# Cross attention before a six-layer transformer: biases added by VectorE and GpSimd, kB cleared at the start, x fetched in two adjacent transfers

## The chip, the cores and the metric

The kernel runs on one core of a Trainium2 chip. A core has five engines that work side by side and meet through semaphores: TensorE (PE; its weight loads are shown as PEld), VectorE (DVE), ScalarE (ACT), GpSimd (POOL) and SyncE (SP), which here only issues DMAs. The metric is the device time in microseconds (us). The kernel before has a median of 1854.88 us over 3 runs (1846.59 to 1856.06). All arithmetic is float32.

## The reference

```
x:[4,512,128]  ctx:[4,77,128]
xn = layernorm(x)
q = xn @ Wq.T + bq;  k = ctx @ Wk.T + bk;  v = ctx @ Wv.T + bv
attended = softmax(q k^T / sqrt(128)) @ v
x = x + tanh(g_xattn) * ((xn + attended) @ Wo.T + bo)
z = layernorm(x)
for 6 layers:
    z = local attention(shift(z); 16 heads of 64, window 32, rotary tables) + z
    z = gated FFN(layernorm(shift(z))) + z
x = x + tanh(g_ffn) * z
```

The change is in the first three steps, the cross attention. The biases bv and bo are no longer zero in the data, so they have to be added.

## The kernel before, in words

The program has a prologue (the cross attention and the second layernorm) and then a software-pipelined loop over 192 units, 8 for each of 24 groups (6 layers times 4 batch rows), with 22 slots to drain. The loop isn't touched. Each engine has its program written out by hand; nothing plans the order.

The prologue works by batch row b = 0 to 3, each with 4 tiles of 128 tokens (TPG = 4). Its steps, with the lines of the code:

- SP fetches, in this order (L1107 to L1120): the first half of x (b 0 and 1), the identity and the mask, ctx, four weights, bq, bk, bv, bo, the two gates, the second half of x (b 2 and 3), the rotary constants `rope`; then the scales, the layer weights and some bias columns.
- PE turns the four weights and ctx (L284, L287), ACT copies them out of PSUM (L574, L576).
- Layernorm of x: for each b, DVE takes statistics (L761, L764), POOL computes 1/sqrt(var + eps) in two small instructions (L1018, L1020), DVE normalises with four `tensor_scalar` (L771). DVE's order is statistics 0, statistics 1, normalise 0, statistics 2, normalise 1, and so on. When POOL has done all four b it clears kB (L1023: 128 x 8704 float32), the buffer of the loop's keys.
- PE turns the normalised rows (L293), ACT copies (L581), PE computes keys (L298) and queries (L303), ACT adds bk and bq as it copies (L585, L589), PE computes the scores (L307).
- DVE takes the maxima and subtracts them (L784, L786). PE meanwhile computes v (L313, L314): for each b, a product of a row of ones with the row bv opens the PSUM bank, and the product of ctx and Wv is accumulated on it. ACT copies v out (L592) and, behind that in its program, does the four exponentials (L595).
- DVE sums, inverts and scales the probabilities (L789 to L793), PE turns them (L321) and multiplies by v (L326), DVE adds xn (L797).
- For each b PE turns the sum (L332) and then writes bo into the bank of the output with a one-row product of 128 x 512 (L334); after all four, the output projection accumulates on it (L339).
- DVE computes x + tanh(g) times the bank (L803) and runs the second layernorm with the same routines; POOL has the same two small instructions per b, then multiplies the rotary tables by the scales (L1029, four instructions of 128 x 256), waits for PE's last transpose (L345) and clears `vw` (L1031), whose space the prologue used for weights.
- ACT copies the transposes into xT (L604, L605), and the loop begins with L370.

The new names of the change: `bias_x` and `bo_t` lie in the tile `rstd`, which the loop uses only later; `cols_zero` takes over what `zero_ready` said of the tile `cols`.

Of the kernel before, what the change touches and what calls it, by code (L numbers as in the profile page):

```python
# [66 lines left out]
def build(nc, x_in, ctx_in, g_xattn, g_ffn, Wq, bq, Wk, bk, Wv, bv, Wo_x, bo, Wqkv, q_scale, k_scale,  # L67
          Wo, ln_g, ln_b, W1, b1, W2, b2, rope_in, mats_in, mask_in, out):
    ctx = ExitStack()
    with ctx:  # L70
# [65 lines left out]
        bcol = sb("bcol", [P, 2])  # L136
        brow = sb("brow", [1, 2, C])
        ones = sb("ones", [1, P])
        gcol = sb("gcol", [P, 2])
# [15 lines left out]
        mv_x = [quad(small(b, 24, 2 * TPG), 2) for b in range(B)]  # L155
        vare_x, rstd_x, mx_x, rs_x, rr_x = ([small(b, 32 + 4 * i, TPG) for b in range(B)] for i in range(5))
        first_bank = [ps[2 * b] for b in range(B)]
        second_bank = [ps[2 * b + 1] for b in range(B)]
# [14 lines left out]
        cst_ready = sem("cst_ready")  # L173
        zero_ready = sem("zero_ready")
        w1_pad = sem("w1_pad")
        vw_zero = sem("vw_zero")
# [29 lines left out]
        a_rTev = sem("a_rTev")  # L206
        a_y = sem("a_y")
        a_x1 = sem("a_x1")
        b_stat = sem("b_stat")
# [69 lines left out]
        def _(pe):  # L279
# [10 lines left out]
            for b in range(B):  # L290
                pe.wait_ge(a_xn, 4 * b + 4)
                for t in range(TPG):
                    mm = pe.transpose(first_bank[b][:, t * P:(t + 1) * P], xn_x[b][:, t, :], ident[:, :])  # L293
                mm.then_inc(a_xnT, 1)
                if b == 0:
                    pe.wait_ge(ctxT_ev, 1)
                    pe.wait_ge(cst_ready, 4)
                    pe.matmul(ps[7][:, 0:B * CTX], wxT[:, 1, :], ctxT[:, :, :].rearrange("p b s -> p (b s)"),  # L298
                              start=True, stop=True).then_inc(kx_mm, 1)
# [4 lines left out]
            for b in range(B):  # L304
# [4 lines left out]
                mm.then_inc(a_sc, 1)  # L309
            pe.wait_ge(small_dma, 16 * 6)  # L310
            for b in range(B):
                o_ = ps[7][0:CTX, b * C:(b + 1) * C]
                pe.matmul(o_, ones[0:1, 0:CTX], brow[0:1, 0, :], start=True, stop=False)  # L313
                mm = pe.matmul(o_, ctxT[:, b, :], wxT[:, 2, :], start=False, stop=True)  # L314
            mm.then_inc(vx_mm, 1)
# [13 lines left out]
            for b in range(B):  # L329
                pe.wait_ge(a_res, b + 1)  # L330
                for t in range(TPG):
                    mm = pe.transpose(second_bank[b][:, t * P:(t + 1) * P], res_x[b][:, t, :], ident[:, :])  # L332
                mm.then_inc(a_rT, 1)
                pe.matmul(heads(first_bank[b][:, :], C), ones[0:1, :],  # L334
                          brow[0:1, 1, :].unsqueeze(1).to_broadcast([1, TPG, C]), start=True, stop=True)
            for b in range(B):
                pe.wait_ge(a_rTev, b + 1)
                for t in range(TPG):
                    mm = pe.matmul(first_bank[b][:, t * P:(t + 1) * P], rT_x[b][:, t * P:(t + 1) * P], wxT[:, 3, :],  # L339
                                   start=False, stop=True, skip_group_check=True)  # L340
                mm.then_inc(a_y, 1)
            for b in range(B):
                pe.wait_ge(b_x, 4 * b + 4)
                for t in range(TPG):
                    mm = pe.transpose(second_bank[b][:, t * P:(t + 1) * P], x_nat[b][:, t, :], ident[:, :])  # L345
                mm.then_inc(b_xT, 1)
            pe.matmul(SC_BANK[:, :], mean_w[:, :], rT_x[1], start=True, stop=True).then_inc(sc_open, 1)

# [223 lines left out]
        def _(act):  # L572
# [3 lines left out]
            act.activation(ctxT[:, :, :].rearrange("p b s -> p (b s)"), ps[7][:, 0:B * CTX], ACT.Copy).then_inc(ctxT_ev, 1)  # L576
            act.wait_ge(cst_ready, 4)
            act.wait_ge(mats_dma, 16 * 2)
            for b in range(B):
                act.wait_ge(a_xnT, b + 1)  # L580
                act.activation(xnT_x[b], first_bank[b][:, :], ACT.Copy).then_inc(a_xnTev, 1)  # L581
                if b == 0:
                    act.wait_ge(small_dma, 16 * 6)
                    act.wait_ge(kx_mm, 1)
                    act.activation(kxT[:, :, :].rearrange("p b s -> p (b s)"), ps[7][:, 0:B * CTX], ACT.Identity,  # L585
                                   bias=bcol[:, 1:2]).then_inc(kx_ev, 1)
            for b in range(B):
                act.wait_ge(a_q, b + 1)
                act.activation(q_x[b], second_bank[b][:, :], ACT.Identity, bias=bcol[:, 0:1]).then_inc(a_qev, 1)  # L589
            act.activation(tg[:, :], gcol[:, :], ACT.Tanh).then_inc(tanh_ready, 1)  # L590
            act.wait_ge(vx_mm, 1)
            act.activation(vx[:, :, :].rearrange("p b c -> p (b c)"), ps[7][0:CTX, :], ACT.Copy).then_inc(vx_ev, 1)  # L592
            for b in range(B):
# [156 lines left out]
        def _(dve):  # L750
            dve.memset(ones[:, :], 1.0).then_inc(cst_ready, 1)
            dve.memset(minus_half[:, :], -0.5).then_inc(cst_ready, 1)
            dve.memset(shift_back[:, :], 0.5 * float(np.log(LN_SHIFT))).then_inc(cst_ready, 1)
            dve.memset(norm_min[:, :], NORM_MIN ** 2)
            dve.memset(mean_w[:, :], 1.0 / C).then_inc(cst_ready, 1)
            dve.memset(xT[64:C, :, 0:1], 0.0)

            def statistics(b, src, stat):
# [16 lines left out]
            for b in range(B + 1):  # L775
                if b < B:
                    dve.wait_ge(x_dma[b // 2], 16)
                    statistics(b, row, a_stat)
                if b > 0:
                    normalise(b - 1, row, xn_x, a_stat, a_rstd, a_xn)  # L780
            for b in range(B):
                dve.wait_ge(a_sc, b + 1)
                sc = heads(first_bank[b][:, :], P)[:, :, 0:CTX]
                dve.tensor_reduce(mx_x[b], sc, AX.X, ALU.max).then_inc(a_mx, 1)  # L784
                dve.wait_ge(a_mx, b + 1)
                dve.tensor_tensor(pr_x[b], sc, spread(mx_x[b], CTX), ALU.subtract).then_inc(a_sub, 1)  # L786
            for b in range(B):
                dve.wait_ge(a_exp, b + 1)
# [5 lines left out]
            for b in range(B):  # L794
                dve.wait_ge(a_att, b + 1)
                dve.wait_ge(a_xn, 4 * b + 4)
                dve.tensor_tensor(res_x[b], heads(first_bank[b][:, :], P), xn_x[b], ALU.add).then_inc(a_res, 1)  # L797
            dve.wait_ge(tanh_ready, 1)
            for b in range(B + 1):
                if b < B:  # L800
                    rows = x1[:, TPG * b:TPG * (b + 1), :]
                    dve.wait_ge(a_y, b + 1)
                    dve.scalar_tensor_tensor(out=rows, in0=heads(first_bank[b][:, :], P), scalar=tg[:, 0:1],  # L803
                                             in1=rows, op0=ALU.mult, op1=ALU.add).then_inc(a_x1, 1)
# [204 lines left out]
        def _(pool):  # L1009
            pool.memset(cols[:, :, :], 0.0).then_inc(zero_ready, 1)  # L1010
            pool.memset(w1[:, 2 * DFF:], 0.0).then_inc(w1_pad, 1)
            pool.wait_ge(cst_ready, 3)

# [8 lines left out]
            inverse_roots(a_stat, a_rstd)  # L1022
            pool.memset(kB[:, :, :, :], 0.0).then_inc(zero_ready, 1)  # L1023
            inverse_roots(b_stat, b_rstd)

            pool.wait_ge(cst_dma, 16)
            pool.wait_ge(scale_dma, 16 * 6)
            for t in range(TPG):
                pool.tensor_tensor(tables[:, 0, t, :], rope[:, t, :], scales[:, 0, :], ALU.mult).then_inc(table_ready, 1)  # L1029
            pool.wait_ge(b_xT, B)  # L1030
            pool.memset(free, 0.0).then_inc(vw_zero, 1)  # L1031
# [72 lines left out]
        def _(sp):  # L1104
            xt = x_in.rearrange("b (t p) c -> p (b t) c", p=P)
            half = B * TPG // 2
            sp.dma_start(x1[:, 0:half, :], xt[:, 0:half, :]).then_inc(x_dma[0], 16)  # L1107
            sp.dma_start(ident[:, :], mats_in).then_inc(mats_dma, 16)
            sp.dma_start(mask_f[:, :, :], mask_in).then_inc(mats_dma, 16)
# [4 lines left out]
            sp.dma_start(bcol[:, 1:2], bk.unsqueeze(1)).then_inc(small_dma, 16)  # L1114
            sp.dma_start(brow[:, 0, :], bv.unsqueeze(0)).then_inc(small_dma, 16)
            sp.dma_start(brow[:, 1, :], bo.unsqueeze(0)).then_inc(small_dma, 16)
            sp.dma_start(gcol[:, 0:1], g_xattn.unsqueeze(0).to_broadcast([P, 1])).then_inc(small_dma, 16)
            sp.dma_start(gcol[:, 1:2], g_ffn.unsqueeze(0).to_broadcast([P, 1])).then_inc(small_dma, 16)
            sp.dma_start(x1[:, half:, :], xt[:, half:, :]).then_inc(x_dma[1], 16)
            sp.dma_start(rope[:, :, :], rope_in).then_inc(cst_dma, 16)  # L1120
# [20 lines left out]
            second_weights(0)  # L1141
            sp.wait_ge(zero_ready, 1)
            with nc.allow_non_contiguous_dma(reason="a few bias columns"):
# [99 lines left out]
```

## Time and profile before

| | |
|---|---|
| runs | 1856.06, 1854.88, 1846.59 us |
| the profiled execution: its own time | 1855.28 us |
| its span (first to last instruction shown) | 1853.5 us |
| mean granted TensorE clock | 0.982 |
| busy | PE 96%, PEld 61%, DVE 87%, ACT 72%, POOL 81% |
| the loop's first instruction | 81.02 us after the span's start |

Busy shares are means over the whole span. The loop holds some 1770 of its 1853.5 us, so these shares speak of the loop; the prologue has to be read from its own stretch, 0 to 81 us. The chain of waits is the view to read first there: it follows the work that ended last back to what released it, so an edit counts only with what it takes off that chain.

### The profile page before, as it was taken

The numbers are of one execution on the slowest core, as the hardware profiler recorded it, in microseconds if no ns is written. First come the engines' busy times: TensorE is split into PE (matmuls) and PEld (weight loads), VectorE is DVE, ScalarE is ACT, GpSimd is POOL, SyncE is SP. The second block draws the span as 40 slices with busy tenths as digits, with TensorE's granted clock in tenths as the row PEclk, the third lists the DMA queues.
The fourth block names the chain that finished last, engine by engine and source line by source line (L and its number), as shares of the span: only waits on it lengthen the run. The fifth ranks groups of instructions, "written<-read, shape, count | busy, mean of one in ns | idle before, by whom it ended". The sixth has DMA issues, their size and how long they took to land.

```text
span 1853.5 us, 48613 instructions
## 1 busy us (share of the span) xinstructions
PE 1770.5 (96%) x18100; PEld 1122.9 (61%) x18100; DVE 1621.2 (87%) x2780; ACT 1327.3 (72%) x2363; POOL 1497.1 (81%) x1200
## 2 busy tenths in 40 slices
PE   5789999999999999999999999999999999999986
PEld 4446666666666666666666666666666666666663
DVE  5499989899989999899899998999998998988873
ACT  2267778677777687787787777787877877877763
POOL 2399988888888888889888888888888888888760
PEclk9699999999999999999999999999999999999998
DMA  4013222223222223222222222222232222222221
GB/s 106 15 44 85 74 56 69 64 56 82 71 67 68 63 58 83 64 73 70 56 63 74 72 74 60 67 61 73 71 80 57 69 61 56 59 72 56 56 64 29
DMA packets 154989, 120.46 MB, mean 65 GB/s; under 512 B 42577, under 2 KB 151173, under 8 KB 154629
## 3 DMA queue, kind: packets, MB, share of 16 engines
q1 hardware_dynamic: 154757, 117.35, 24.5%
q8 instruction: 147, 2.41, 0.6%
q14 instruction: 85, 0.70, 0.1%
HBM read 18.66 MB, written 1.05 MB: 11 GB/s over the span
## 4 chain that ended last, share of the span: by engine, by line
PE 77%; DVE 11%; POOL 4%; issue 3%; SPq 2%; DMA 1%; ACT 1%; DVEq 0%; POOLq 0%; ACTq 0%
PE qk_bank L370 17%; PE ring_bank L442 10%; PE ring_bank L466 9%; PE ring_bank L383 8%; PE sc_bank L417 7%; PE ring_bank L510 6%; PE ring_bank L430 4%; PE ring_bank L393 3%; PE ring_bank L455 3%; PE ring_bank L521 3%; PE ring_bank L404 3%; DVE rn L832 2%; DVE step L827 2%; DVE o L888 2%; POOL turned L1039 1%
## 5 line engine op out<-in xcount | busy, mean ns | idle before, releaser
L1039 POOL TENSOR_TENSOR turned<-qkn,tables 128x512 f32<-128x512 f32 x384 | 489.1, 1274 | 210.8 <-DVE qkn L840 203.1
L1046 POOL TENSOR_TENSOR turned<-qkn,tables 128x512 f32<-128x512 f32 x384 | 497.3, 1295 | 0.0
L370 PE MATMUL qk_bank<-wqkv,xT 128*128 128x512 f32 x768 | 368.7, 603 | 16.8 <-DVE qkn L848 16.8
L1075 POOL TENSOR_TENSOR turned<-turned 128x512 f32<-128x512 f32 x192 | 255.0, 1328 | 15.1
L1082 POOL TENSOR_TENSOR turned<-turned 128x512 f32<-128x512 f32 x192 | 244.9, 1276 | 15.1
L442 PEld LDWEIGHTS ring_bank<-vw,pT 128*32 128x32 f32 x6144 | 156.6, 110 | 143.8 <-issue 143.7
L650 ACT ACTIVATE kB<-ring_bank 64x512 f32<-64x512 f32 x384 | 225.4, 587 | 23.3 <-PE ring_bank L404 20.9
L623 ACT ACTIVATE vs<-ring_bank 128x512 f32<-128x512 f32 x192 | 114.7, 597 | 173.3 <-PE ring_bank L383 158.5
L814 DVE TENSOR_REDUCE ss<-sq 128x16 f32<-128x1024 f32 x192 | 232.0, 1208 | 7.7 <-ACT sq L614 7.7
L888 DVE TENSOR_TENSOR o<-ring_bank,rr 128x512 f32<-128x512 f32 x192 | 132.0, 687 | 107.3 <-PE ring_bank L442 104.8
L383 PE MATMUL ring_bank<-wqkv,xT 128*128 128x512 f32 x384 | 217.2, 648 | 1.6 <-DVE x L968 1.6
L417 PE MATMUL sc_bank<-kB,qT 128*32 128x128 f32 x6144 | 208.4, 276 | 0.1
L442 PE MATMUL ring_bank<-vw,pT 128*32 128x128 f32 x6144 | 208.4, 276 | 0.1
L660 ACT ACTIVATE sc_bank<-mask_f 128x512 f32<-128x512 f32 x192 | 114.5, 596 | 131.2 <-DVE pr L863 130.8
L370 PEld LDWEIGHTS qk_bank<-wqkv,xT 128*128 128x128 f32 x768 | 132.0, 192 | 120.5 <-issue 94.4
L614 ACT ACTIVATE sq<-qk_bank 128x1024 f32<-128x1024 f32 x192 | 198.0, 1031 | 0.0
L417 PEld LDWEIGHTS sc_bank<-kB,qT 128*32 128x32 f32 x6144 | 156.6, 110 | 34.9 <-issue 34.8
L466 PE MATMUL ring_bank<-oT,wo 128*128 128x256 f32 x768 | 173.8, 379 | 0.0
L455 PEld LDWEIGHTS ring_bank<-ident,o 128*128 128x128 f32 x768 | 95.8, 141 | 101.8 <-issue 84.2
L466 PEld LDWEIGHTS ring_bank<-oT,wo 128*128 128x128 f32 x768 | 142.2, 190 | 18.1 <-DVE uT L946 0.8
L510 PE MATMUL ring_bank<-xnT,w 128*128 128x512 f32 x288 | 143.2, 609 | 8.5 <-DVE xnT L937 7.3
L840 DVE TENSOR_TENSOR qkn<-qk_bank,rn 128x512 f32<-128x512 f32 x192 | 132.8, 692 | 20.0
(173 smaller groups left out, 3149.5 us busy)
## 6 DMA issues: line engine op xcount, KB each, us to landing
vw<-vs SPq DMA_DIRECT2D x1152, 64.0 KB, 2.1
vw<-vs SPq DMA_DIRECT2D x672, 32.0 KB, 1.9
wqkv<-in_L_ffn_Wqkv_dram SPq DMA_DIRECT2D x20, 384.0 KB, 3.5
wo<-in_L_ffn_Wo_dram SPq DMA_DIRECT2D x20, 128.0 KB, 3.3
w<-in_L_ffn_W_dram SPq DMA_DIRECT2D x6, 341.0 KB, 3.4
wqkv<-in_L_ffn_Wqkv_dram SPq DMA_DIRECT2D x1, 1536.0 KB, 10.3
x<-in_x_dram SPq DMA_DIRECT2D x2, 512.0 KB, 4.1
out_dram<-x SPq DMA_DIRECT2D x4, 256.0 KB, 2.3
```

The source lines that it names most:

```text
L370: mm = pe.matmul(QK[u % 2][:, i * UW:(i + 1) * UW], tok, wqkv[:, layer % 2, cut:cut + UW], start=True, stop=True)
L383: pe.matmul(RING[i % RINGS][:, :], xT[:, b, t * P:(t + 1) * P], wqkv[:, layer % 2, cut:cut + UW], start=True, stop=True).then_inc(ring_mad ...
L417: mm = pe.matmul(heads(SC_BANK[WIN * w:WIN * (w + 1), k * P:(k + 1) * P]), qT[:, u % 2, k, WIN * w:WIN * (w + 1)], kB[:, HP * half + k, :, ...
L442: mm = pe.matmul(heads(RING[i % RINGS][WIN * w:WIN * (w + 1), k * P:(k + 1) * P]), pT[:, u % 2, k, WIN * w:WIN * (w + 1)], vw[:, u % 2, w, ...
L466: mm = pe.matmul(RING[i % RINGS][:, 0:HALF], wo[:, layer % 2, k, :], oT[:, k, HALF * h:HALF * (h + 1)], start=(k == 0), stop=(k == KO - 1))
L510: pe.matmul(RING[i % RINGS][:, :], w1[:, DFF * j + k * P:DFF * j + (k + 1) * P], xnT[:, :], start=True, stop=True).then_inc(ring_made[i % ...
L650: ev = act.activation(kB[64 * h:64 * h + 64, HP * half:HP * half + HP, h, WIN + P * t:WIN + P * t + P], RING[i % RINGS][64 * h:64 * h + 64 ...
L814: dve.tensor_reduce(ss[:, :], heads(sq[:, :]), AX.X, ALU.add).then_inc(ss_done, 1)
L1039: return pool.tensor_tensor(heads(turned[:, u % 2, 2 * i, :]), heads(qkn[:, u % 2, i * UW:(i + 1) * UW]), table.unsqueeze(1).to_broadcast( ...
L1046: return pool.tensor_tensor(halves(turned[:, u % 2, 2 * i + 1, :]), halves(qkn[:, u % 2, i * UW:(i + 1) * UW])[:, :, ::-1, :], table.rearr ...
L1075: pool.tensor_tensor(q, q, turned[:, u % 2, 1, :], ALU.add).then_inc(q_summed, 1)
L1082: pool.tensor_tensor(k, k, turned[:, u % 2, 3, :], ALU.add).then_inc(k_summed, 1)
```

## The change

It does four things.

1. v: the four products of ones and bv go. DVE adds bv, spread over the partitions by the DMA, as it copies v out of PSUM; ACT's copy of v goes. This addition stands on DVE behind the four subtractions (L786).
2. Output: the four products of ones and bo go. DVE multiplies bo (spread over the partitions by the DMA) by tanh(g) once, and POOL adds the result to x itself, 128 x 512 for each b, before the projection's result is added to x. The tanh moves forward on ACT, behind the copy of the keys. POOL multiplies the rotary tables before these additions, and no longer after the second layernorm's roots.
3. kB is cleared first thing: a quarter of it by DVE (2176 of 8704 columns), the rest by POOL (6528), and no longer behind the first layernorm's roots.
4. SP issues the second half of x directly behind the first.

```
--- before
+++ after
@@ PE
-                    pe.wait_ge(cst_ready, 4)
-            pe.wait_ge(small_dma, 16 * 6)
             for b in range(B):
-                o_ = ps[7][0:CTX, b * C:(b + 1) * C]
-                pe.matmul(o_, ones[0:1, 0:CTX], brow[0:1, 0, :], start=True, stop=False)
-                mm = pe.matmul(o_, ctxT[:, b, :], wxT[:, 2, :], start=False, stop=True)
+                mm = pe.matmul(ps[7][0:CTX, b * C:(b + 1) * C], ctxT[:, b, :], wxT[:, 2, :], start=True, stop=True)
...
-                pe.matmul(heads(first_bank[b][:, :], C), ones[0:1, :],
-                          brow[0:1, 1, :].unsqueeze(1).to_broadcast([1, TPG, C]), start=True, stop=True)
...
-                                   start=False, stop=True, skip_group_check=True)
+                                   start=True, stop=True)
@@ ACT
+                    act.activation(tg[:, :], gcol[:, :], ACT.Tanh).then_inc(tanh_ready, 1)
...
-            act.activation(tg[:, :], gcol[:, :], ACT.Tanh).then_inc(tanh_ready, 1)
-            act.wait_ge(vx_mm, 1)
-            act.activation(vx[:, :, :].rearrange("p b c -> p (b c)"), ps[7][0:CTX, :], ACT.Copy).then_inc(vx_ev, 1)
@@ DVE
-            dve.memset(ones[:, :], 1.0).then_inc(cst_ready, 1)
+            dve.memset(kB[:, 0:2, :, :], 0.0).then_inc(zero_ready, 1)
...
+            dve.wait_ge(small_dma, 16 * 6)
+            dve.wait_ge(tanh_ready, 1)
+            dve.tensor_scalar(bo_t, bias_x[:, 1, :], tg[:, 0:1], None, ALU.mult).then_inc(bo_ready, 1)
...
+            dve.wait_ge(vx_mm, 1)
+            dve.tensor_tensor(vx[:, :, :], heads(ps[7][0:CTX, :], C),
+                              bias_x[0:CTX, 0, :].unsqueeze(1).to_broadcast([CTX, B, C]), ALU.add).then_inc(vx_ev, 1)
...
+                    dve.wait_ge(bo_added, b + 1)
@@ POOL
-            pool.memset(cols[:, :, :], 0.0).then_inc(zero_ready, 1)
+            pool.memset(cols[:, :, :], 0.0).then_inc(cols_zero, 1)
+            pool.memset(kB[:, 2:, :, :], 0.0).then_inc(zero_ready, 1)
-            pool.wait_ge(cst_ready, 3)
+            pool.wait_ge(cst_ready, 1)
             inverse_roots(a_stat, a_rstd)
-            pool.memset(kB[:, :, :, :], 0.0).then_inc(zero_ready, 1)
-            inverse_roots(b_stat, b_rstd)
             pool.wait_ge(cst_dma, 16)
             pool.wait_ge(scale_dma, 16 * 6)
             for t in range(TPG):
                 pool.tensor_tensor(tables[:, 0, t, :], rope[:, t, :], scales[:, 0, :], ALU.mult).then_inc(table_ready, 1)
+            pool.wait_ge(bo_ready, 1)
+            for b in range(B):
+                rows = x1[:, TPG * b:TPG * (b + 1), :]
+                pool.wait_ge(a_xn, 4 * b + 4)
+                pool.tensor_tensor(rows, rows, bo_t.unsqueeze(1).to_broadcast([P, TPG, C]), ALU.add).then_inc(bo_added, 1)
+            inverse_roots(b_stat, b_rstd)
@@ SP
+            sp.dma_start(x1[:, half:, :], xt[:, half:, :]).then_inc(x_dma[1], 16)
...
-            sp.dma_start(brow[:, 0, :], bv.unsqueeze(0)).then_inc(small_dma, 16)
-            sp.dma_start(brow[:, 1, :], bo.unsqueeze(0)).then_inc(small_dma, 16)
+            sp.dma_start(bias_x[:, 0, :], bv.unsqueeze(0).to_broadcast([P, C])).then_inc(small_dma, 16)
+            sp.dma_start(bias_x[:, 1, :], bo.unsqueeze(0).to_broadcast([P, C])).then_inc(small_dma, 16)
...
-            sp.dma_start(x1[:, half:, :], xt[:, half:, :]).then_inc(x_dma[1], 16)
```

## Rows read from the trace of the kernel before

**Rows 1.** The page: the granted clock in 40 equal slices of the span.
```profile
PEclk9699999999999999999999999999999999999998
```

**Rows 2.** The chain of waits, 0 to 81 us: start, us, what.
```profile
7.04 4.16 DMA x<-in_x_dram
...
16.18 7.93 DVE oT L771 x4
...
24.16 1.11 PE ring_bank L293 x4
...
33.47 0.37 PE ring_bank L313 x2
...
38.16 0.49 DVE oT L793
...
43.16 3.41 PE qk_bank L326 x16
...
49.99 0.85 PE qk_bank L332 x4
50.84 2.00 PE qk_bank L334 x2
52.84 1.04 PE qk_bank L332 x4
...
61.98 2.02 PE qk_bank L339 x8
...
75.56 2.80 DVE oT L771 x4
```

**Rows 3.** Instructions in order of time, 0 to 24 us: start, us, engine, line.
```profile
1.00 0.17 DVE L755 MEMSET mean_w<- 128x128 f32 x1
...
4.72 0.87 DVE L761 BATCH_NORM_STATS2 xnT<-x 128x6 f32<-128x128 f32 x4 [3.43 <-DMA x<-in_x_dram]
...
7.39 1.08 PE L284 MATMUL ring_bank<-ident,vw 128*128 128x128 f32 x4 [7.39 <-DMA vw<-in_L_xattn_Wo_dram]
...
7.58 1.11 DVE L771 TENSOR_SCALAR oT<-x,xnT 128x128 f32<-128x128 f32 x4 [0.40 <-POOL xnT L1020]
...
9.56 1.38 SPq L1128 DMA_DIRECT2D scales<-in_L_ffn_k_scale_dram  x3
...
10.07 1.24 PE L298 MATMUL ring_bank<-vw 128*128 128x308 f32 x2
...
14.62 1.08 DVE L771 TENSOR_SCALAR oT<-x,xnT 128x128 f32<-128x128 f32 x4
...
16.10 7.35 POOL L1023 MEMSET kB<- 128x8704 f32 x1
```

**Rows 4.** The same view, 24 to 79 us.
```profile
25.06 3.16 PE L303 MATMUL qk_bank<-oT,vw 128*128 128x512 f32 x4
...
28.06 1.88 PE L303 MATMUL ring_bank<-oT,vw 128*128 128x512 f32 x4
...
34.03 0.48 DVE L786 TENSOR_TENSOR oT<-ring_bank,xnT 128x308 f32<-128x308 f32 x1
...
36.47 0.59 ACT L592 ACTIVATE vw<-ring_bank 77x512 f32<-77x512 f32 x1 [5.72 <-PE ring_bank L314]
...
50.02 0.69 DVE L797 TENSOR_TENSOR oT<-ring_bank,oT 128x512 f32<-128x512 f32 x1 [1.02 <-PE ring_bank L326]
...
75.50 2.77 POOL L1029 TENSOR_TENSOR tables<-rope,scales 128x256 f32<-128x256 f32 x4
```

**Rows 5.** Busy time by stretch: stretch, sum, PE, PEld, DVE, ACT, POOL, clock, DMA share, GB/s.
```profile
3.00:4.00 1.00, 0.00 (x0) 0.00 (x0) 0.00 (x0) 0.00 (x0) 0.00 (x0) 1.00 1.15 347
...
46.00:48.00 2.00, 2.00 (x11) 2.00 (x11) 0.69 (x1) 0.00 (x0) 0.00 (x0) 0.50 0.00 0
...
90.00:100.00 10.00, 8.77 (x20) 4.15 (x20) 8.85 (x10) 4.41 (x10) 9.77 (x9) 0.71 0.23 59
```

**Rows 6.** DMA issues by line, whole span: count, KB each, median us to landing.
```profile
scales<-in_L_ffn_k_scale_dram SPq DMA_DIRECT2D x12, 16.0 KB, 4.8
```

More of the change, by code:

```diff
@@ L136, in build @@
         bcol = sb("bcol", [P, 2])
-        brow = sb("brow", [1, 2, C])
-        ones = sb("ones", [1, P])
         gcol = sb("gcol", [P, 2])
@@ L156, in build @@
         vare_x, rstd_x, mx_x, rs_x, rr_x = ([small(b, 32 + 4 * i, TPG) for b in range(B)] for i in range(5))
+        bias_x = rstd[:, 0:2 * C].rearrange("p (i c) -> p i c", c=C)
+        bo_t = rstd[:, 2 * C:3 * C]
         first_bank = [ps[2 * b] for b in range(B)]
@@ L174, in build @@
         zero_ready = sem("zero_ready")
+        cols_zero = sem("cols_zero")
         w1_pad = sem("w1_pad")
@@ L207, in build @@
         a_y = sem("a_y")
+        bo_ready = sem("bo_ready")
+        bo_added = sem("bo_added")
         a_x1 = sem("a_x1")
@@ L346, in _ @@
                 mm.then_inc(b_xT, 1)
+            pe.wait_ge(cst_ready, 3)
             pe.matmul(SC_BANK[:, :], mean_w[:, :], rT_x[1], start=True, stop=True).then_inc(sc_open, 1)
@@ L576, in _ @@
             act.activation(ctxT[:, :, :].rearrange("p b s -> p (b s)"), ps[7][:, 0:B * CTX], ACT.Copy).then_inc(ctxT_ev, 1)
-            act.wait_ge(cst_ready, 4)
+            act.wait_ge(cst_ready, 3)
             act.wait_ge(mats_dma, 16 * 2)
@@ L797, in _ @@
                 dve.tensor_tensor(res_x[b], heads(first_bank[b][:, :], P), xn_x[b], ALU.add).then_inc(a_res, 1)
-            dve.wait_ge(tanh_ready, 1)
             for b in range(B + 1):
@@ L1141, in _ @@
             second_weights(0)
-            sp.wait_ge(zero_ready, 1)
+            sp.wait_ge(cols_zero, 1)
             with nc.allow_non_contiguous_dma(reason="a few bias columns"):
```

## The prediction

> **What bounds the kernel now.** I read the page first. Its shares (PE busy 96%) belong to the loop, which the change doesn't touch, and its row of the granted clock [rows 1] has 0.6 in the slice from 46 to 93 us and 0.9 in nearly all others. So the question is how much earlier the loop begins than at 81 us. The chain of waits comes second, for 0 to 81 us. The reader is to see five things in it [rows 2]: the chain waits until 11.2 us for the second half of x (issued at 7.04, landed 4.16 later); four normalising instructions take 7.93 us at 16.18; PE then carries it, with the v products from 33.47 to where ACT's copy starts, 36.47 [rows 4]; from 49.99 to 64.00 PE alternates transposes and one-row products of 2.00 each; and at 75.56 four normalising instructions take 2.80. The instructions in order of time come third and say why [rows 3, 4]: the same four take 1.08 at 14.62, but at 16.10 POOL began to clear kB for 7.35 us, until 23.45, and DVE's began at 16.18 and one ended just behind it. At 75.50 it is the rotary tables, 2.77 us on POOL. I read both as DVE's instruction held off while POOL's runs.
>
> The Trainium skill (SBUF — State Buffer, Who interferes with whom) says the same of a two-port DVE instruction beside any GpSimd instruction, and that a DVE instruction with one SBUF input at most, outside these modes, isn't held. By that, DVE's share of the new clearing runs free beside POOL's; no row of before shows it, and the last rival is what it would be otherwise.
>
> **Part A: x earlier, kB cleared at the start.** POOL's new clearing has 6528 of 8704 columns: 0.75 x 7.35 = 5.5 us [rows 3]. It begins near 1.0 and ends near 6.5. DVE's has 2176 columns; at the 0.17 us of 128 columns [rows 3] that is 2.9 us at most, fixed part counted 17 times, so it ends by 4.2, before x lands at 4.72: cost 0. POOL's roots for b 0 could start at about 6.2 before, now 6.5; normalise 0 starts at 7.9 for 7.58. The second half of x, issued about 1.2, has landed well before DVE wants it at about 9. DVE then goes without a gap: statistics 2, normalise 1 (from 10.2), statistics 3 (11.2), normalise 2 (12.4). From normalise 2 to normalise 3 the trace has 16.18 - 14.62 = 1.56 (it waits for POOL's root), so normalise 3 starts at 13.9 and ends at 15.0 where it ended at 24.11.
>
> Can PE follow? The second half goes ahead of the weights: 512 KB at 347 GB/s [rows 5] put 1.5 us on their arrival, 7.39 becomes 8.9 [rows 3]. From the weights' first transpose to the end of the key product took 11.31 - 7.39 = 3.9, now ends about 12.8; the transposes of b 1 and 2 (1.11 each, [rows 2]) follow, and b 3 starts at 15.1. A near tie; I take 15.1 for 24.16: gain 9.0. Bounds: 9.2 if PE is no limit, 7 if the weights come 2 us later still (the 4.16 of a whole half-x transfer instead of 1.5, less the slack). The other DMAs that are moved back (identity, mask, ctx, weights, six small ones) are wanted no earlier than this; the small ones, two of them longer now, gate the copy of the keys at about 13.
>
> The tables move to POOL's idle time behind its roots (13.9). They wait for the scales, whose last issue ended at 10.94 [rows 3] and which take 4.8 to land [rows 6]: 15.7 before, about 16 now, so normalise 3 (13.9 to 15.0) is just ahead of them. If they came earlier it would cost what it costs now at 75.5, 2.80 - 1.08 = 1.7; that end goes into the range. POOL's four additions: a 256-column instruction takes 2.77 / 4 = 0.69 [rows 4], so 512 columns 1.4, four of them 5.6: POOL is through at 16 + 2.8 + 5.6 = 24.4, and the first projection's result waits for them near 44. Cost 0; if that cover went it would be 5.6. In that time DVE waits for scores; its multiplication of bo (below 0.7) may be held by a table, unseen.
>
> **Part B: v.** Eight PE instructions go, a pair for each b, 4 x 0.37 = 1.5 [rows 2]. In the old clock times: v is ready at 34.95 for 36.45. DVE has finished its last subtraction at 34.51 [rows 4]. ACT's exponentials no longer stand behind its copy of v (0.59 from 36.47), so all four are done when DVE arrives. DVE adds bv: a 128 x 512 addition out of PSUM takes 0.69 [rows 4], to 35.7; then sum, reciprocal, product for b 0, 1.2 us, end at 36.9. Before it was 38.65 [rows 2]. Gain 1.75; the next steps are paced by DVE as before. Bounds: 1.5 (the products alone) and 2.0.
>
> **Part C: output.** The chain from the end of the last attention product (49.99) to the first projection's end (64.00) is four transposes groups (0.85 and three of 1.04), four one-row products of 2.00 and a projection of 2.02 [rows 2]: 14.0. Without the products: 3.4 to 4.0 of transposes, 1.7 to 2.0 of projection, 5.1 to 6.0. DVE's addition of b 3 (0.69 at 50.02, [rows 4]) and ACT's copies fit beneath. Gain 8.0 to 8.9; I take 8.5. What follows is DVE's chain (14.3 us from 64.09 to 78.36), which needs the projections of b 1 to 3 at 2 to 3 us' distance: PE delivers them each 1.7.
>
> **Part D: tables out of the way.** The last normalise of the second layernorm is 2.80 - 1.08 = 1.7 shorter [rows 2, 3]. Bounds 0 and 1.7. The clearing of `vw` stays where it is in the order.
>
> **Sum.** 9.0 + 1.75 + 8.5 + 1.7 = 20.95, say 21. The loop's weights have long landed at 60 us, so it starts 21 us earlier. The profiled execution took 1855.28, 0.4 over the median of the runs: 1855.3 - 21 = 1834.3, as a median about 1834.
>
> **The rivals.**
>
> *More, by the clock.* In the prologue PE works at 1.2 GHz from about 38 to 64 us (the row at 46 has 0.50, [rows 5]), and at the start too: the first four query instructions take 3.16, the next four 1.88 at the other level, 2.4 GHz, though the clock shows 1.00 there [rows 4]. Before it fell, PE had stood idle from the end of v (36.45) to 38.70. Now PE is fed more densely from 9 to 16 us and stands 2.0 instead of 2.3 us before the probabilities; and the one-row products are gone from the stretch in which the clock stayed low. If the clock is high throughout: queries 1.3, attention products half of 6.8, transposes 1.7, projection 0.9: 7.3 more, 1827. For: the denser work. Against: PE stood fully busy at 46 with the clock at 0.50, and the 2.0 us stand remains. The Trainium skill (TensorE: Matmul & The Clock Gate, What's actually happening) has the slow level as the default that sustained activity releases; that would favour this rival, while the busy row at 46 doesn't agree with it taken as busy share alone. Chance 0.22.
>
> *Less, at the start.* DVE's clearing is held by POOL's: it starts at 6.5, ends at 8.8 to 9.4, and statistics 0 begins 4.4 later than 4.72. Normalise 0 would follow two statistics (2.4) at about 11.5 instead of 7.9, so the first part gives 5.5 and the total 17.4: 1838. The tables meeting normalise 3 (1.7) or late weights (2) end in the same place. For: the row at 16.18 shows a DVE instruction held for POOL's whole clearing. Against: clearing reads nothing. Chance 0.18.
>
> *Slower, the loop gives it back.* The loop starts at another point of the clock's and the DMAs' course. Its first 30 us ran mostly at the high level; if the low one held from the loop's start on, PE's work there would double. From 90 to 100 us PE is busy 8.8 of 10 at a mean clock of 0.71 [rows 5], so 6.2 of work at the full one, which would take 12.5 at the low one: with the 0.71 that it had already, some 4 more for each 10 us, up to 6 where the clock was high. The 21 us are used up when this lasts for about 40 us, and at 50 it is 1859. For: the median and the best run of the same kernel lie 8 us apart, so the loop can take different courses. Against: in the page's row all slices but the second and the last are at 9 [rows 1]. Chance 0.04.
>
> *It doesn't do what it says.* The chain's 9 us at the start are replaced by another wait (scales or biases late, and with them POOL's additions): for this the landing would have to be over 20 us late. With small gains elsewhere, no change: 1846 to 1855. Chance 0.04.
>
> **How the numbers follow.** The forecast as summed has 0.52, with a range of its own of 1830 to 1838 (the bounds of the parts). The first rival reaches to 1826, the second to 1841. 1824 to 1842 leaves out the last two rivals and the edges of the others, under 2 in 10. A change of 0.5% (9 us) is what a measurement can tell from none: faster 0.93, same 0.04, slower 0.03.
>
> **What would show it.** Right: normalise 3 ends near 15 and each normalise group takes 1.08; the second half of x is no longer in the chain; the scores begin near 21 and the probabilities' first product ends near 28; the gap from the last attention product to the first projection's end is 5 to 6; the loop's first instruction is near 60; from there on the trace is as before. Wrong: DVE's clearing longer than 3 us or ending after 4.7; a wait of PE for the weights beyond 10 us; the loop from its first instruction to the end longer or shorter than 1772 us by more than 5, which would say that the prologue isn't all of it.

## The result and the profile after

The changed kernel takes 1826.74 us (median of 4 runs, 1823.28 to 1829.92); the kernel before, with one run more than was shown, 1850.88 (1846.59 to 1856.06). The ratio is 0.9868, 95% interval 0.983 to 0.9906. Five further rounds (t1 below) gave 0.9877, 0.9864 to 0.9891. It is faster, by about 24 us; 21 were forecast.

The two profiled executions split it. In the chain of waits the loop's first products began at 81.23 us before and at 56.94 after: 24.3 us less. From there to the end of the span it was 1772.3 us before and 1771.0 after. So the gain is all in the prologue, and the loop, which wasn't touched, carried it through.

The chain of waits of the changed kernel (start, us, what):

```profile
7.85 1.12 DVE oT L767 x4
...
14.09 0.87 DVE oT L767 x3
...
15.00 1.02 PE ring_bank L296 x4
16.02 1.72 PE qk_bank L305 x4
...
24.03 0.59 DVE vw L787
...
31.13 3.41 PE qk_bank L325 x16
...
36.25 1.71 PE ring_bank L325 x8
37.95 1.71 PE qk_bank L331 x8
39.66 0.95 PE ring_bank L331 x8
40.61 0.91 PE qk_bank L336 x8
...
53.00 1.13 DVE oT L767 x4
...
56.94 1.72 PE qk_bank L368 x4
```

The transfer of x's second half is gone from the chain; it now begins with POOL's clearing of kB, which holds up the first root by 0.3 us. L767 is the normalising instruction (L771 before); at 14.09 and 53.00 the groups of four that took 7.93 and 2.80 us [rows 2] take 1.1 each. The first queries take 1.72 us for four instructions (the profile shows a float32 product as two instructions, so these are the products of b 0 and 1); in the chain of before they took 2.95 (3.16 in the other view, [rows 4]). Between the last attention product (ends 37.96) and the first projection's end (41.52) there are 3.56 us; there were 14.0 [rows 2].

The same kernel's instructions in order of time (start, us, engine, line; in brackets the idle time before and what ended it):

```profile
0.88 5.54 POOL L1014 MEMSET kB<- 128x6528 f32 x1
...
1.71 1.87 DVE L752 MEMSET kB<- 128x2176 f32 x1 [0.50 <-issue]
1.84 1.56 SPq L1115 DMA_DIRECT2D ident<-in_mats_dram  x1
...
4.89 0.88 DVE L757 BATCH_NORM_STATS2 xnT<-x 128x6 f32<-128x128 f32 x4 [1.31 <-DMA x<-in_x_dram]
...
9.15 1.08 PE L287 MATMUL ring_bank<-ident,vw 128*128 128x128 f32 x4 [9.15 <-DMA vw<-in_L_xattn_Wo_dram]
...
19.46 2.78 POOL L1029 TENSOR_TENSOR tables<-rope,scales 128x256 f32<-128x256 f32 x4 [5.67 <-DMA scales<-in_L_ffn_k_scale_dram]
...
22.20 5.18 POOL L1034 TENSOR_TENSOR x<-x,rstd 128x512 f32<-128x512 f32 x4
...
25.25 1.01 DVE L795 TENSOR_TENSOR oT<-oT,xnT 128x308 f32<-128x308 f32 x1
...
28.35 0.48 DVE L795 TENSOR_TENSOR oT<-oT,xnT 128x308 f32<-128x308 f32 x1
```

Two things are to be seen. DVE's clearing ended at 3.58, in the middle of POOL's: it wasn't held. And DVE's product of the probabilities (L795) took 1.01 us while POOL added bo, and 0.48 when POOL was through. That wait is new. The product began at 25.25 and ended at 26.26, 0.4 behind the end of POOL's third addition (24.66 to 25.92); the next one (26.89 to 27.72) ended 0.3 behind the end of the fourth. It works the other way too: POOL's fourth addition took 1.51 us, the three before it 1.27.

### The profile page after: what moved, and what is told of

Same layout as the page of the kernel before. It is cut to its first block, busy times and chain, and to the rows that moved or that the text cites. A ratio compares the mean times of both kernels' runs of the same rounds, so it can differ in the third digit from the quotient of the medians.

```text
span 1827.9 us, 48590 instructions
## 1 busy us (share of the span) xinstructions
PE 1753.5 (96%) x18084; PEld 1118.2 (61%) x18084; DVE 1614.7 (88%) x2782; ACT 1326.9 (73%) x2362; POOL 1500.5 (82%) x1204
## 3 DMA queue, kind: packets, MB, share of 16 engines
HBM read 18.79 MB, written 1.05 MB: 11 GB/s over the span
## 4 chain that ended last, share of the span: by engine, by line
PE 79%; DVE 11%; POOL 4%; issue 2%; SPq 2%; DMA 1%; ACT 1%; DVEq 0%; POOLq 0%; ACTq 0%
PE qk_bank L368 17%; PE ring_bank L440 10%; PE ring_bank L464 9%; PE ring_bank L381 8%; PE sc_bank L415 8%; PE ring_bank L508 6%; PE ring_bank L428 4%; PE ring_bank L391 4%; PE ring_bank L453 3%; PE ring_bank L402 3%; PE ring_bank L519 3%; DVE rn L834 2%; DVE step L829 2%; DVE o L890 2%; DVE qkn L850 1%
```

## The experiments

Each was run once, with a profile, beside the kernel before, so the times of e1 to e9 are of single executions; the last three of the table were run in five rounds, and their times are medians. "Prologue" is the start of the loop's first products in the chain of waits, "loop" the rest of the span, all in us.

| kernel | prologue | loop | first four queries | time |
|---|---|---|---|---|
| before | 81.2 | 1772.3 | 2.95 | 1850.88 median of 4 |
| after | 56.9 | 1771.0 | 1.72 | 1826.74 median of 4 |
| e1, kB cleared first | 74.8 | 1772.7 | 3.29 | 1849.37 |
| e2, x second | 78.5 | 1767.7 | 2.91 | 1848.06 |
| e3, bo alone | 72.2 | 1771.6 | 2.97 | 1845.82 |
| e4, after, tables last | 57.8 | 1772.0 | 1.72 | 1831.86 |
| e5, after, additions before tables | 56.4 | 1771.8 | 1.72 | 1830.28 |
| e6, after, PE fed | 53.0 | 1766.2 | 2.96 | 1821.20 |
| e7, after, 128 rows | 54.8 | 1767.4 | 1.72 | 1824.14 |
| e8, after, e5 to e7 together | 52.9 | 1769.6 | 3.02 | 1824.54 |
| e9, before, 128 rows | 75.7 | 1770.8 | 3.33 | 1848.32 |
| t1, after again | 57.5 | 1771.4 | 1.72 | 1829.24, ratio 0.9877 (0.9864 to 0.9891) |
| t2, e6 again | 52.2 | 1770.2 | 1.72 | 1824.60, ratio 0.9852 (0.9838 to 0.9865) |
| t3, e8 again | 51.1 | 1767.8 | 1.72 | 1821.39, ratio 0.9842 (0.9829 to 0.9855) |

The loop took 1766 to 1773 us whatever the prologue was: because of that spread a single time can't tell effects of a few us, while the prologue in the trace can.

**e1, e2: is DVE held by POOL's clearing, and does either edit do it alone?**

```
e1  kB cleared at the start by both engines, as in the change; nothing else
e2  sp.dma_start(x1[:, half:, :], ...) moved behind the first half; nothing else
```

> The kernel before with kB cleared first thing by DVE and POOL, the order of x as before. Theory (DVE's normalise is held by POOL's clearing): the last normalise of the first layernorm takes 1.1 us instead of 7.9, still behind x's second half (11.2), so it ends at 17.3 and the loop's first product comes 6.8 us earlier than 81.2 in the chain, at 74.4. Rival (the 7.9 us have another cause, such as the wait for POOL's root): they stay, and nothing is gained. On the clock: PE stands from 11.3 to 13.6 as before, so the first query products stay at 0.74 us each; if they come at 0.43, it is the transposes' distance that counts, and the gain is 8.

> The kernel before with only the second half of x issued second. Theory: normalise 3 now meets POOL's clearing earlier (from about 13.7 to 21.1) and ends at 21.2 instead of 24.1, so only 2.9 of the 4.2 us of the earlier x arrive, loop at 78.3. Rival (x's place alone is the gain): normalise 3 takes 1.1 us, ends at 15, and the gain is 9 to 10. With e1, the two edits give 6.8 and 2.9 alone and 9.2 together, a sum only by accident: either alone leaves the other's wait.

The chain of e1, and then that of e2:

```profile
16.21 1.12 DVE oT L773 x4
...
18.50 3.29 PE qk_bank L304 x4
```
```profile
13.47 7.93 DVE oT L771 x4
```

Both came near what the theory had: e1 6.4 us less for 6.8, e2 2.8 for 2.9. With x early but kB cleared where it was, the same four instructions take the same 7.93 us, only earlier, so the clearing is the cause of the 7.93. The two edits take off different pieces and nearly add up. Up to the start of the transposes of b 3 (24.16 before, 17.38 in e1, 21.45 in e2, 15.00 in the changed kernel) they bring 6.8 and 2.7 alone and 9.2 together: an early x is worth 2.7 with the clearing in its old place and 2.4 (17.38 to 15.00) with it away. Neither of the two hides the other.

**e3: is the output's gain the products' own 8 us, or more?**

```
-                pe.matmul(heads(first_bank[b][:, :], C), ones[0:1, :], brow[0:1, 1, :]..., start=True, stop=True)
...
in words: bo * tanh(g) on DVE, four additions to x on POOL behind its clearing of kB
```

> The kernel before with bo alone moved: multiplied by DVE, added to x by POOL behind its clearing of kB, the four one-row products gone; v, kB, x and the tables as before. Theory (the one-row products cost 8 us on the chain, and they also keep the clock low): from the last attention product to the first projection's end 3.6 us instead of 14.0, gain 10.4, with the transposes of b 2 and 3 already at 0.13 us instead of 0.21 a piece. Rival (the products' own time alone): 5.5 to 6, gain 8 to 8.5, the clock rising only where the projection runs, as in the changed kernel it would then have come from another stretch (PE denser from 9 us on).

```profile
49.89 1.71 PE ring_bank L330 x8
51.60 1.69 PE qk_bank L336 x8
53.29 0.87 PE ring_bank L336 x8
54.16 0.91 PE qk_bank L341 x8
```

In this chain the last attention products end at 51.60; eight transposes take 1.69, the next eight 0.87, and the projection is done at 55.07: 3.5 us for 14.0, and the clock rises between the two halves of the transposes, as in the changed kernel. The start of e3 is as before (a transfer of x even landed 1.6 us later), so the rise isn't owed to the denser work at the start. The theory stands: 10.5 us, 8 of them the products' own. Of the other 2.5, the clock's part is some 1.6 by an estimate: the second eight transposes and the projection of b 0 take 0.87 and 0.91, and eight transposes at the low level 1.7. The rest isn't split further.

**e4, e5: POOL's two-input work beside DVE.**

```
e4   tables behind inverse_roots(b_stat, b_rstd) again
e5   the four additions of bo ahead of the tables
```

> The changed kernel with the rotary tables behind the second layernorm's roots again. Theory (part D: DVE's last normalise is held by the tables): it takes 2.8 us instead of 1.13, loop's first product at 58.6 instead of 56.9. A second effect: POOL's four additions of bo then start at about 15.2, not 22.2, and are through at 20.4, so the products of the probabilities (1.01 and 0.84 us in the changed kernel) take 0.48 again and the first step gains 0.9: in total 57.7. Rival (no hold, the 1.7 us of before were something else): 56.9 or, with the second effect, 56.0.

> The changed kernel with POOL's additions of bo ahead of the rotary tables. Theory (DVE's product of probabilities reads two tensors in SBUF and is held by a POOL addition): POOL adds from 15.2 to 20.4, all four products of the probabilities take 0.48 us, and the loop's first product comes 0.9 us earlier, at 56.0. Rival (the products were long for another reason, ACT's or PE's access): 1.01 and 0.84 stay, 56.9. Tables then at 20.4 to 23.2 could at most hold the addition of bv (one SBUF input beside PSUM: not expected).

The chains of e4 and of e5:

```profile
24.88 0.48 DVE oT L795
...
52.16 2.80 DVE oT L767 x4
```
```profile
24.89 0.48 DVE oT L795
...
52.44 1.13 DVE oT L767 x4
```

e4 brought the 2.80 back and e5 left it at 1.13: the tables do hold DVE's last normalise, and part D was worth 1.7. In both POOL adds earlier (15.22 to 20.16 in e5), and the products of the probabilities take 0.48. So the new wait is POOL's additions. The prologue of e5 was only 0.5 us shorter than that of the change, for 0.9 expected, though PE reached its attention products at 29.89 instead of 31.13: the clock rose near 40 us in both (mean 0.54 and 0.58 from 38 to 40 us), so an earlier start of the same work ran longer at the low level.

**e6, e7, e8: can the low level between the queries and the projection be had back?**

```
e6   behind v:  2 x pe.matmul(second_bank[0][:, :], mean_w[:, :], q_x[i], start=True, stop=True)
     behind the transposes of b 0 and 1:  pe.matmul(second_bank[b + 1][:, 0:2 * P], mean_w[:, :], q_x[3][:, 0:2 * P], ...)
e7   -  pT_x[b][0:CTX, ...], vx[:, b, :]
     +  pT_x[b][:, ...], vx_all[:, b, :]      with vx_all cleared by DVE at the start
e8   e5, e6 and e7 together
```

> The changed kernel with PE given products whose result nobody reads: two of 128 x 512 behind v, one of 128 x 256 behind the transposes of the probabilities of b 0 and of b 1. Theory (PE's stand of 2.4 us and its half-empty time with the probabilities let the clock fall): the clock stays at 2.4 GHz, the attention products take 0.106 us apiece instead of 0.213, 3.4 us less for 32, and transposes and projection another 1: loop's first product at 52.5. Rival (the attention products, over 77 of 128 rows, let it fall or don't hold it themselves): they start at 0.106 and go to 0.213 on their way, gain 1 to 2.

> The changed kernel with the attention products over 128 rows instead of 77: v has 51 rows of zeros, cleared by DVE at the start, and the transposed probabilities have the queries' values there. Same instruction count and columns. Theory (a PE that is fully busy with 77 rows doesn't raise the clock, one with 128 rows does): the clock rises within the 32 attention products, about half of them at 0.106 us, gain 1.7 to 2.5, loop's first product at 54.5 to 55.2. Rival (rows don't matter, the clock rises when it would anyway, near 39.3 us): nothing changes, 56.9.

> The changed kernel with the three edits of e5, e6 and e7 together. Theory: additions ahead of the tables 0.9, and the clock at 2.4 GHz from the queries to the projection: attention products 3.4, transposes 0.8, projection 0: sum 5.1, loop's first product at 51.8. If e6 alone keeps the clock up, e7 adds nothing here; if e7 alone does, e6 adds what the probabilities' stretch gives, up to 0.5.

The chain of e6, then the attention products of e7 in order of time:

```profile
16.11 2.96 PE qk_bank L305 x4
...
31.56 1.79 PE qk_bank L330 x16
```
```profile
30.85 3.62 PE L327 MATMUL qk_bank<-vw,uT 128*128 128x128 f32 x16
...
34.27 1.46 PE L327 MATMUL sc_bank<-vw,uT 128*128 128x128 f32 x8
...
35.56 1.06 PE L327 MATMUL ring_bank<-vw,dT 128*128 128x128 f32 x8
```

Fed, PE kept the high level: the 32 instructions of the 16 attention products took 3.57 us instead of 6.83, and e6 was 3.9 us shorter although its queries ran at the low level this time. In e7, over 128 rows, the clock rose among the products themselves; in the chain its last eight instructions took 0.89. e7 came out inside its range. e8 missed its 51.8 in its first execution (52.9, queries at the low level) and beat it in the next (51.1, t3).

**e9: the same 128 rows in the kernel before.**

```
     pT_x[b][:, ...], vx_all[:, b, :]   in the kernel before; the one-row products stay behind it
```

> The kernel before with only the attention products over 128 rows (v with 51 rows of zeros, cleared by DVE at the start). Theory (128 busy rows raise the clock where 77 don't): the clock is at 2.4 GHz before the 32 products end, 1.5 to 2.5 us less for them; but the one-row products stand behind them, and if these don't hold the clock it falls again within them, so the first projection's end comes 2 to 5 us earlier. If they hold it, all of the output step runs at the high level, 7 us less. Rival (rows don't matter, e7's early rise was chance): attention products 6.8 us as before.

Instructions of PE in order of time:

```profile
43.44 2.96 PE L328 MATMUL qk_bank<-vw,uT 128*128 128x128 f32 x16
46.24 1.06 PE L328 MATMUL sc_bank<-vw,uT 128*128 128x128 f32 x8
...
48.56 1.12 PE L336 MATMUL qk_bank<-brow,ones 1*128 1x512 f32 x2
...
51.83 1.56 PE L336 MATMUL sc_bank<-brow,ones 1*128 1x512 f32 x2
...
54.37 2.07 PE L336 MATMUL ring_bank<-brow,ones 1*128 1x512 f32 x2
```

Busy time by stretch (stretch, sum, PE, PEld, DVE, ACT, POOL, clock, DMA share, GB/s):

```profile
46.00:48.00 2.00, 2.00 (x20) 2.00 (x19) 1.44 (x3) 0.00 (x0) 0.00 (x0) 1.00 0.00 0
...
52.00:54.00 2.00, 2.00 (x5) 0.80 (x6) 0.00 (x0) 0.54 (x1) 0.00 (x0) 0.60 0.00 0
54.00:56.00 2.00, 2.00 (x5) 0.53 (x3) 0.00 (x0) 0.60 (x1) 0.00 (x0) 0.50 0.00 0
```

This is the run that says most about the clock. The clock rose to 1.00 within the 128-row products and fell to 0.50 within the one-row products, with PE busy 2.00 of every 2.00 us throughout. The attention products took 4.5 us instead of 6.8, a one-row product of 128 x 512 (two instructions) 1.05 at the high level and 2.00 once the clock had fallen, and the first projection ended 5.5 us earlier than before, a little past the range of the theory. In the kernel before PE was as busy from 40 us on, over 77 rows and then over one, and stayed at 0.50 until 64 us. The 51 added rows of v are zeros; whether it is the number of rows or something else about them that counts, no run here separates.

**t1, t2, t3: do the prologue's gains arrive?**

> The changed kernel once more, unchanged, beside the next two on the same chip. Theory (the prologue is 24 us shorter, the loop as long as before within 5 us either way): ratio to before 0.986 to 0.989. Rival (the loop has a share in the gain): under 0.984.

> The kernel of e6 (PE given unread products around the probabilities), timed. Theory: the 3.9 us that its prologue was shorter than the changed kernel's (53.0 for 56.9) arrive, ratio to before 0.002 under t1's. Rival (the clock's level in the loop's ramp depends on the moment and gives it back): same as t1 within 0.001.

> The kernel of e8 (additions ahead of the tables, PE fed, 128 rows), timed. Theory: 4.1 us under t1 as in its prologue (52.9 for 56.9), with the query products at the high level in some executions 1.3 more: ratio 0.002 to 0.003 under t1's. Rival: as for t2. It isn't to be told from t2.

They do. t1 lies within its range. t2 is 4.6 us under t1 (0.0025 in the ratio) and t3 7.9 (0.0035, a little more than the 0.002 to 0.003 expected), where their prologues are 5.3 and 6.4 shorter; the loop of t3's profile was 3.6 shorter as well, within the loop's spread. The intervals of t1 and t3 don't touch, those of t1 and t2 just do (0.9864 and 0.9865). The version of e8, with all three edits, beats both kernels: 0.9842 of before.

## Why the prediction was right

**Part A.** 9.0 forecast, 9.16 measured (24.16 to 15.00); e1 and e2 show the mechanism. DVE's clearing cost nothing, as taken. The weights came at 9.15 for 8.9: behind two half-x transfers SP needed 1.56 us to issue the identity. PE and DVE met at 15.0 in the near tie that was forecast.

**The queries.** Not in the sum: 1.3. PE worked nearly without a break from 9 us, and the clock was up when the queries began (1.72 us for four instead of 2.95). Here the first rival was right in part. It isn't sure in every execution: of nine with the change's early order, seven had it and two (e6, e8) didn't, while none of the five with the late clearing or the late x did. What decides stays open: e6 and t2 are the same kernel, and one ran them at the low level, the other at the high one.

**Part B.** 1.75 forecast, 1.54 measured (the end of the probabilities' transposes against the scores' start: 43.16 - 29.94 before, 31.13 - 19.45 after). The step that failed is "POOL is through at 24.4" and "cost 0". The scales were taken to land 4.8 us after their last issue [rows 6], a median over the whole span; in before's own prologue the six transfers took 4.3 to 6.8, and here POOL waited from 13.8 until 19.46, 7.1 behind the end of the last issue. POOL's additions thus ran to 27.4 instead of 24.4, into DVE's products of the probabilities, which read two tensors in SBUF. I had looked for holds on the four normalises alone. The Trainium skill (SBUF — State Buffer, Who interferes with whom) has it: a DVE instruction with two SBUF inputs contends with a GpSimd instruction that reads SBUF. The trace agrees, 1.01 for 0.48; the prediction had quoted the page's other half. The two long products cost 0.53 and 0.36. That B lost only 0.2 by it is luck: 0.7 came back because v was ready when DVE's last subtraction ended, where 0.44 of waiting was forecast, because the addition of bv was 0.1 shorter, and the three steps behind it, but for the wait, 0.1 shorter together.

**Part C.** 8.5 forecast, 10.5 measured. The 8 us of the products are right; the rest of the step was mis-sized, 5.5 expected and 3.56 measured. Some 1.6 of that is the clock, since the transposes and the projection were taken at the low level all through, and 0.4 is that the lower end of the stated 5.1 to 6.0 fits the low level, not the middle. e3 gives the same 10.5 alone.

**Part D.** 1.7 forecast, 1.7 measured (14.37 - 12.65 between the first projection and the transposes of b 3), undone by e4.

**Sum.** 9.16 + 1.33 + 1.54 + 10.48 + 1.72 = 24.2, against 24.3 in the traces; the forecast's 20.95 lacks 1.3 in the queries and 2.0 in the output, nearly all of it the clock's, and has 0.2 too much in B and 0.2 too little in A. The median of 1826.74 lies 7.3 under the forecast: 3.3 by that, the other 4 because the median of before, from which the forecast subtracted, was 1854.88 then and 1850.88 with one run more. So the mechanism of the four parts was right, the clock's share was missed, and that the median lies at the 1827 of the first rival is chance: that rival wanted 7.3 us from the clock, and some 2.9 came (1.3 and 1.6).

**The rivals.** "Less, at the start": no, DVE's clearing wasn't held, and the measured start says so. "Slower": no, the loop took 1766 to 1773 us in 14 profiles, whatever its start. "More, by the clock": of its four terms the queries and the projection came, the transposes by half, the attention products not at all, and e6 shows that they can. "It doesn't do what it says": no; though the scales were late, POOL's additions ended at 27.4 and the first projection at 41.5.

## What to carry to other kernels

Before sharing work out to POOL, list for its whole duration what DVE runs beside it: in these traces a DVE product over two SBUF tensors (1.01 us for 0.48) or a `tensor_scalar` within SBUF (7.93 and 2.80 for 1.1) ended only behind the end of the POOL instruction that ran when it began, while DVE's statistics, its clearing and what it read from PSUM went on. Only POOL's long instructions did this, the clearing, the tables and the additions: beside a root of 128 x 4 (1.04 us, at 15.11 in the kernel before) four normalises took their 1.08 [rows 3]. When two edits shorten the same stretch, run each alone and read the trace at the same point: here they nearly add (6.8 and 2.7 alone, 9.2 together). Bias rows on PE as one-row products are not cheap: one of 512 columns took 1.05 us at the high level, where a query product of 512 columns over 128 rows took 0.86, and 2.00 at the low one, and in e9 the clock fell among them. An engine that idles can take the addition over at little cost, but its place there counts: behind the tables POOL's additions held DVE for 0.9 us, ahead of them for nothing.

## What was not expected of the hardware

In these traces the busy share of PE doesn't tell the granted clock. The Trainium skill (TensorE: Matmul & The Clock Gate, What's actually happening) has activity release the slow level; what the traces show is that a PE which is busy without a break may still stay at it, or fall to it. With PE busy all the time, it stayed at 0.50 over 77-row products in all eight profiles in which PE wasn't fed before them (31.1 to 37.9 us in the changed kernel), rose within 128-row ones in both profiles that ran these from the low level (35.1 us in e7, 45.6 in e9, worked out from the mean clock of their 2 us stretches), and fell within one-row ones (52.4 in e9). Where PE was fed and came to the 77-row products at 1.00, it stayed there through their 3.6 us (e6, t2). In the changed kernel it rose behind the last 77-row product, within the 128-row transposes:

```profile
36.00:38.00 2.00, 2.00 (x12) 2.00 (x11) 0.70 (x2) 0.00 (x0) 0.00 (x0) 0.50 0.20 36
38.00:40.00 2.00, 2.00 (x12) 2.00 (x11) 0.69 (x1) 0.90 (x2) 0.00 (x0) 0.58 0.00 0
40.00:42.00 2.00, 2.00 (x20) 2.00 (x19) 0.46 (x1) 1.29 (x3) 0.00 (x0) 1.00 0.00 0
```

The granted clock reads 1.00 at the very start of a trace although the instructions take the time of the low level (four query instructions 2.95 us before, 1.72 at the high one): up to the first change of level the durations have to be read there, not that column.
